# Feature tiles that pair heads of two units, in the linear-attention part of an attention and mixture-of-experts kernel

## The reference

```python
def taylor_feature_map(x):
    iu, ju = jnp.triu_indices(d)
    quad = x[..., iu] * x[..., ju] * scale
    return jnp.concatenate([ones, x, quad], axis=-1)
...
def step(carry, inp):
    kv, ksum = carry
    A = jnp.einsum('bchf,bshf->bhcs', qb, kb) * causal
    y = jnp.einsum('bhcs,bshd->bchd', A, vb) + jnp.einsum('bchf,bhfd->bchd', qb, kv)
    z = jnp.einsum('bhcs->bch', A) + jnp.einsum('bchf,bhf->bch', qb, ksum)
    kv = kv + jnp.einsum('bshf,bshd->bhfd', kb, vb)
    ksum = ksum + kb.sum(axis=1)
    return ((kv, ksum), y / (z[..., None] + EPS_LIN))
```

## Time and profile before

| what | us |
|---|---|
| median of three runs | 480.66 |
| profiled execution, whole | 480.37 |
| its span, first to last instruction | 478.6 |
| attention, first L640 to the last copy L839 | 49.0 to 282.1 |
| PE busy in the span | 406.1 |
| DVE busy | 290.9 |
| ACT busy | 206.2 |
| POOL busy | 179.2 |

### The profile page before, as it was taken

How to read it: one execution, slowest core, us unless ns; L and a number is a source line. 1 busy time by engine, 2 the same in 40 slices (tenths; PEclk the granted TensorE clock), 3 DMA queues, 4 the chain that set the end, 5 groups by cost and what they waited for, 6 DMA issues and landing times. The chain is left out here.

```text
span 478.6 us, 14438 instructions
## 1 busy us (share of the span) xinstructions
PE 406.1 (85%) x4869; PEld 272.9 (57%) x4869; DVE 290.9 (61%) x1178; ACT 206.2 (43%) x502; POOL 179.2 (37%) x305
## 2 busy tenths in 40 slices
PE   0787999999999999999999961599998999999830
PEld 0455777777776677777777640245555555555420
DVE  5575454667756667666675647256665666666614
ACT  0465455445554555554455530044444444444420
POOL 5444433454454554555544345003222222223220
PEclk9999999999999999999999995599999999999975
DMA  7556755444455444423223700211110111111008
GB/s 203 134 142 175 213 136 151 112 112 139 144 165 135 120 120 142 121 66 82 51 53 85 258 14 32 71 42 36 45 38 28 29 43 37 31 34 34 18 16 251
DMA packets 91624, 46.14 MB, mean 96 GB/s; under 512 B 56410, under 2 KB 89852, under 8 KB 91554
## 3 DMA queue, kind: packets, MB, share of 16 engines
q1 hardware_dynamic: 88562, 40.50, 31.8%
q0 software_dynamic: 2272, 4.46, 2.5%
q10 hardware_dynamic: 720, 0.26, 0.2%
HBM read 33.67 MB, written 11.98 MB: 95 GB/s over the span
## 5 line engine op out<-in xcount | busy, mean ns | idle before, releaser
L1097 DVE TENSOR_REDUCE mrow<-ps 128x4 f32<-128x512 f32 x64 | 44.2, 691 | 73.9 <-PE ps L604 73.9
L1303 POOL TENSOR_SCALAR_AFFINE_SELECT amat<-amat 128x512 f32<-128x512 f32 x64 | 42.1, 657 | 119.6 <-ACT amat L819 119.3
L1325 POOL DMA_INDIRECT results<-qas,mrowid x39 | 38.1, 978 | 126.2 <-ACT qas L879 123.1
L747 PE MATMUL ps<-wgl,rest 128*128 (+1 forms) x156 | 75.3, 605 | 4.7 <-DVE hT L1186 4.1
L830 ACT ACTIVATE pmat<-ps 128x512 f32<-128x512 f32 x64 | 38.2, 597 | 67.6 <-PE ps L661 67.6
L819 ACT ACTIVATE amat<-ps 128x512 f32<-128x512 f32 x64 | 38.2, 597 | 27.9 <-PE ps L616 27.9
L1186 DVE TENSOR_TENSOR hT<-ps,kv_tok 128x512 f32<-128x512 f32 x39 | 27.0, 691 | 26.5 <-issue 14.6
L747 PEld LDWEIGHTS ps<-wgl,rest 128*128 128x128 f32 x156 | 26.9, 192 | 27.9 <-issue 27.9
L732 PE MATMUL ps<-w,rest 128*128 (+1 forms) x78 | 42.1, 623 | 0.0
L661 PE MATMUL ps<-identb,mneg 128*128 128x128 bf16 x512 | 39.2, 219 | 0.0
L1264 POOL DMA_INDIRECT routed<-routed_row,slot x32 | 32.6, 1018 | 14.0 <-issue 5.8
(11 more groups left out here) (161 smaller groups left out, 834.7 us busy)
## 6 DMA issues: line engine op xcount, KB each, us to landing
qa_parts<-wgl SPq DMA_DIRECT2D x12, 256.0 KB, 3.1
ks<-k_parts SPq DMA_DIRECT2D x32, 96.0 KB
qas<-qa_parts SPq DMA_DIRECT2D x32, 96.0 KB
xin<-routed SPq DMA_DIRECT2D x39, 72.0 KB, 1.9
ks<-k_parts SPq DMA_DIRECT2D x32, 64.0 KB
qas<-qa_parts SPq DMA_DIRECT2D x32, 64.0 KB
w<-in_W SPq DMA_DIRECT2D x2, 1024.0 KB, 5.4
wgl<-in_Wg SPq DMA_DIRECT2D x2, 1024.0 KB, 6.3
```

The costliest lines, as they stand in the source:

```text
L747: t = mm(ps[:, GL, :], zxT[:, k % 2, s, :], rhs(wgl[:, bass.ds(e, 1), s, :]), start=(s == 0), stop=(s == 1))
L1097: v.tensor_reduce(mrow[:], ps[:, SQ, :].rearrange("p (a k) -> p a k", k=CH), AX.X, ALU.max).then_inc(max_done, 1)
L1303: q.affine_select(out=amat[:, u % 2], in_=amat[:, u % 2], compare_op=ALU.is_ge, fill=0.0, base=0, pattern=[[0, 4], [1, CH]], channel_multi ...
L1325: q.indirect_dma_start(results, bass.IndirectOffsetOnAxis(mrowid[:, m:m + 1], 0), yw[:, m, :], None, bounds_check=RESULTS - 1, oob_is_err= ...
```

## The change

Query features of a **pair** of units are now formed at once: tile g (0 to 3) holds head g of the even unit in its first 48 rows and head g of the odd unit in the other 48. L621 runs only before an even unit and writes 512 columns in each of its two products. ACT's square of it (L821) is 96 x 512, once for a pair. The product with `state` (L674 before) is done once for a pair, as four products with 32 weight columns, one for each g, whose outputs lie in the four groups of 32 output rows: the same groups that L679 uses. Keys follow: `u_tok` holds the heads in the new order, each product of L640 takes head g of both units of a pair (values with a stride), and DVE copies KV to `state` once for a pair, in the odd unit. The waits follow the new counts, and SP waits for the scores (`a_ready`) where it waited for the features (`phi_ready`).

```diff
@@ linear_scores
-                if not isinstance(n, int) or n:
-                    pe.wait_ge(phisq_done, n)
-                for par in range(2):
-                    t = mm(ps[0:PR, PHI, 0:2 * CH], sums[:, par, :], as_[:, p, 4 * u + par:4 * u + par + 3:2, :],
-                           start=par == 0, stop=par == 1)
-                t.then_inc(phi_ready, 1)
+                if u % 2 == 0:
+
+                    if n:
+                        pe.wait_ge(phisq_done, n // 2)
+                    for r in range(2):
+                        t = mm(ps[0:PR, PHI, :], sums[:, r, :], as_[:, p, 4 * (u + r):4 * (u + r) + 4, :], start=r == 0, stop=r == 1)
+                    t.then_inc(phi_ready, 1)
@@ chunk, TensorE
-                        if kf or u:
-                            pe.wait_ge(state_done, UNITS * kf + u)
-                        for k in range(2):
...
+                        if u % 2 == 0 and (kf or u):
+                            pe.wait_ge(state_done, 2 * kf + j)
+                        for g in range(2 * hf, 2 * hf + 2):
...
-                    pe.wait_ge(phisq_done, n + 1)
-                    if u % 2 == 0 and pair > 1:
-                        pe.wait_ge(evac_done, pair - 1)
...
-                    for k in range(2):
-                        t = mm(ps[64 * k:64 * k + 64, bank, 0:CH], slot32(state[:, c % 2], 4 * u + 2 * k, 2),
-                               phiq[:, u % 2, k, :], start=u % 2 == 0, stop=False, skip_group_check=True)
-                    t.then_inc(inter_done, 1)
+                    if u % 2 == 0:
+                        pe.wait_ge(phisq_done, pair + 1)
...
+                        for g in range(4):
+                            t = mm(ps[32 * g:32 * g + 32, bank, 0:CH], state[:, c % 2, j, 32 * g:32 * g + 32], phiq[:, pair % 2, g, :],
+                                   start=True, stop=False, skip_group_check=True)
+                        t.then_inc(inter_done, 1)
@@ squares, ScalarE
-                act.wait_ge(phi_ready, n + 1)
-                a_(phiq[:, u % 2].rearrange("p k t -> p (k t)"), ps[0:PR, PHI, 0:2 * CH], ACT.Square).then_inc(phisq_done, 1)
+                if u % 2 == 0:
+                    act.wait_ge(phi_ready, n // 2 + 1)
+                    a_(phiq[:, n // 2 % 2].rearrange("p g t -> p (g t)"), ps[0:PR, PHI, :], ACT.Square).then_inc(phisq_done, 1)
@@ next_state, VectorE
-                        if not later:
+                        if not later or u % 2 == 0:
                             return
@@ load_stack, SyncE
-                    sp.wait_ge(phi_ready, n + 4)
+                    sp.wait_ge(a_ready, n + 4)
```

More of the change, by code:

```diff
@@ L64, in constants @@
     c["blockdiag"] = (blk[:, None] == blk[None, :]).astype(np.float32)
-    sm = np.zeros((PR, 2, 2, UD), np.float32)
-    for par in range(2):
-        sm[par * FS:(par + 1) * FS, :, par] = 1.0
-    c["statemask"] = sm.reshape(PR, 4 * UD)
+    sm = np.zeros((PR, 4, 2, UD), np.float32)
+    for r in range(2):
+        sm[r * FS:(r + 1) * FS, :, r] = 1.0
+    c["statemask"] = sm.reshape(PR, 8 * UD)
     slots = np.zeros((128, 2 * H), np.float32)
@@ L129, in build @@
         blockdiag = sb("blockdiag", [D, D])
-        statemask = sb("statemask", [PR, 4 * UD])
+        statemask = sb("statemask", [PR, 8 * UD])
         epslin = sb("epslin", [128, 2 * H])
@@ L167, in build @@
         v1 = sb("v1", [CH, 2, 2, 2, SLOTW])
-        state = sb("state", [PR, 2, 2, SLOTW])
+        state = sb("state", [PR, 2, 2, CH])
         mrow = sb("mrow", [128, 4])
         mneg = sb("mneg", [128, 2, 2, 4], BF16)
-        phiq = sb("phiq", [PR, 2, 2, CH])
+        phiq = sb("phiq", [PR, 2, 4, CH])
         amat = sb("amat", [CH, 2, 4, CH])
@@ L286, in build, with slot32 @@
         TZX, X12, Y, TO, GL = SQ, ST, A, PHI, OUT0
-        def slot32(tile, h, heads=1):
+        def slot32(tile, h):
             lo = 128 * (h // 4 % 2) + 32 * (h % 4)
[L292 to L296, removed]
+            return tile[:, h // 8, lo:lo + 32]
         def values16(tile, lo, hi):
@@ L634, in chunk @@
                         pe.wait_ge(cross_ready, kf + 1)
-                        if kf or u:
-                            pe.wait_ge(state_done, UNITS * kf + u)
-                        for k in range(2):
[L638 to L642, removed]
+                        if u % 2 == 0 and (kf or u):
+                            pe.wait_ge(state_done, 2 * kf + j)
+                        for g in range(2 * hf, 2 * hf + 2):
+                            at = 4 * j + g
+                            t = mm(ps[0:PR, KV, 2 * at * UD:2 * (at + 1) * UD], phik[:, p, 2 * at:2 * at + 2, :].rearrange("p h f -> p (h f)"),
+                                   v1[:, p, 1, j, :].rearrange("p (r x) -> p r x", r=2)[:, :, 32 * g:32 * g + UD],
+                                   start=c % (T // CH) == 0 and at == 0, stop=True, skip_group_check=True)
                         t.then_inc(kv_ready, 1)
@@ L665, in chunk @@
                     bank = OUT0 + pair % 2
-                    pe.wait_ge(phisq_done, n + 1)
-                    if u % 2 == 0 and pair > 1:
-                        pe.wait_ge(evac_done, pair - 1)
[L669 to L672, removed]
-                    for k in range(2):
-                        t = mm(ps[64 * k:64 * k + 64, bank, 0:CH], slot32(state[:, c % 2], 4 * u + 2 * k, 2),
-                               phiq[:, u % 2, k, :], start=u % 2 == 0, stop=False, skip_group_check=True)
-                    t.then_inc(inter_done, 1)
+                    if u % 2 == 0:
+                        pe.wait_ge(phisq_done, pair + 1)
+                        if pair > 1:
+                            pe.wait_ge(evac_done, pair - 1)
+                        if c % (T // CH):
+                            pe.wait_ge(state_done, 2 * folded(c - 1)[1] + j + 1)
+                        elif c:
+                            pe.wait_ge(state_zeroed, 1)
+                        for g in range(4):
+                            t = mm(ps[32 * g:32 * g + 32, bank, 0:CH], state[:, c % 2, j, 32 * g:32 * g + 32], phiq[:, pair % 2, g, :],
+                                   start=True, stop=False, skip_group_check=True)
+                        t.then_inc(inter_done, 1)
                     pe.wait_ge(amask_ready, n + 1)
@@ L924, in key_features @@
                         dve.wait_ge(phik_ready, kf)
-                    v.tensor_copy(u_tok[:, :, 1:UD], kv_tok[:, c, 0, :].rearrange("p (h d) -> p h d", h=H)).then_inc(us, 1)
+                    v.tensor_copy(u_tok[:, :, 1:UD].rearrange("p (a g r) d -> p a r g d", a=2, g=4),
+                                  kv_tok[:, c, 0, :].rearrange("p (a r g d) -> p a r g d", a=2, r=2, g=4)).then_inc(us, 1)
                 for w in range(2):
@@ L1114, in next_state @@
                     def next_state():
-                        if not later:
+                        if not later or u % 2 == 0:
                             return
+                        a = u // 2
                         dve.wait_ge(kv_ready, UNITS * kf + u + 1)
                         if c:
[L1120 to L1123, removed]
+                            dve.wait_ge(inter_done, 2 * (c - 1) + a + 1)
+                        grf = lambda x: x.rearrange("p (g r f) -> p g r f", g=4, r=2)
+                        v.tensor_tensor(grf(state[:, (c + 1) % 2, a])[:, :, :, 0:UD], grf(ps[0:PR, KV, 8 * a * UD:8 * (a + 1) * UD]),
+                                        grf(statemask[:]), ALU.mult).then_inc(state_done, 1)
                     if n < UNITS * NC - 1:
@@ L1307, in chunk @@
                     if u == 0 and c == T // CH - 1:
-                        pool.wait_ge(inter_done, UNITS * c)
+                        pool.wait_ge(inter_done, 2 * c)
                         q.memset(state[:, (c + 1) % 2], 0.0).then_inc(state_zeroed, 1)
```

## The result

| | before | after |
|---|---|---|
| median of the runs, us | 480.25 (478.96 to 481.72, 4 runs) | 468.45 (467.94 to 469.27, 4 runs) |
| profiled execution, us | 480.37 | 469.27 |
| span, us | 478.6 | 467.1 |

The ratio is 0.9734, 95% interval 0.9704 to 0.9764: 11.8 us faster, against 469.0 forecast, inside the range of 457 to 472. The two profiled executions differ by 11.1 us.

A forecast was written before the change was run, and what follows sets the result against it. PE's own sequence was taken to bound the attention (98% busy). Its 16.7 us saving, cut by holds at chunk borders to 11.3 (5.2 + 5.4 + 0.7), took 480.37 to 469.0 us, range 457 to 472.

The forecast's parts named there:

- L674 in the odd unit: State product on PE in odd units: it goes and nothing replaces it, saving 0.37 us a pair.
- L674 in the even unit: State product joined to L679: one handover (0.37) goes, two sets at 0.11 come, saving 0.15 us a pair.
- L621, nothing: Feature sums, halved in number, doubled in width: even units save 0.22 us, odd ones add 0.22; removed weight loads were hidden.
- The rule of the Trainium skill: Weight loads overlap matmuls only when row groups differ; 64 exposed loads would add 5.8 us saved: 463, chance 0.04.
- The hold, anchored to POOL's chain: Chunk start: L557's wait ends with POOL's indirect DMA, 5.44 us after L616 of u = 2; held chunks give 0.54, not 1.04.
- the time of that exponential: In u = 0 ACT's exponential ends at 212.15, so L691 saves only 0.24 us where it would be 0.37 earlier.
- the tenth border: Chunk 7 to 8: PE 0.44 us earlier against the DMA, hold 0.69 longer (1.24), so the hold ends with the DMA.
- the first rival: Chunk borders: the hold vanishes because L691 ends before the DMA blocks anything; 22.9 us less, 457.5, chance 0.3.
- PE waits for no load: In the attention, SP's later wait costs nothing: the loads queued behind it are for a chunk 15 us away.
- wrong in kind: Sign in the changed kernel's profile that the forecast fails: PE waits for `phiq`, `state` or a load.
- The forecast of 11.3: Total saving in us: five chunks without hold 5.2, ten held 5.4, chunk 15 0.7.
- 16.7 us from PE: Saving on PE if nothing else holds it: 0.52 us a pair, 1.04 a chunk, 32 pairs.

The follow-up runs named there:

- the run with the wide sums alone: Kernel before with feature sums and their square made once per pair of units, state product still one per unit: 473.43 us against 473.67, ratio 0.9975.

## Why the forecast came out right

**L674 in the odd unit, 0.37 a pair: right.** L678 follows L659 directly.

**L674 in the even unit, 0.15 a pair: right.** 0.58 measured for the 0.57 worked out, and the middle set that the trace before did not show costs 0.11, as taken from L621 and L691. The rows left it anywhere between 0.06 and 0.16; the value between was a choice, and it held.

**L621, nothing: right.** L614 to L690 takes 0.33 and 0.76 where 0.33 and 0.77 were worked out, and the run with the wide sums alone is level with the kernel before. The rule of the Trainium skill that spoke against it ("TensorE: Matmul & The Clock Gate", part 3, "The mechanism") has no support here: four loads and two take the same time to 0.01 us.

**The hold, anchored to POOL's chain: right where it stood, and nine times, not ten.** L614 of u = 2 stands at 197.44 and L555 at 202.87:

```profile
197.44 0.40 PE L614 MATMUL ps<-qas,ks 114*128 114x128 bf16 x4
```

That is 5.43, and the forecast had it stay at 5.44. Of the 1.04 us of a chunk, 0.6 was left in six of these nine chunks and 0.35 to 0.50 in three, 0.56 on the mean; 0.54 was forecast. The 0.08 that L614 to L690 takes too long in u = 0 (0.41, the exponential) is part of it, smaller than the 0.13 forecast. The forecast took the time of that exponential as given; it was late because the DMA of u = 0 held the signal that starts it.

**The forecast's reading of the tenth border was wrong.** At chunk 7 to 8 I took the late DMA for a proof that an earlier PE waits longer. There the hold went altogether:

```profile
158.62 0.43 PE L690 MATMUL ps<-pmat,v 128*32 128x64 f32 x16
...
159.37 1.07 POOL L1266 DMA_INDIRECT routed<-routed_row,slot  x1 [0.20 <-issue]
...
159.26 0.26 ACT L838 COPY linT<-ps 128x128 f32<-128x128 f32 x1
```

L690 ended at 159.05, before the DMA began at 159.37, and ACT had copied by then. So the first rival happened once, and gave 2.3 us in that chunk instead of 0.54. The forecast's argument for that rival, that L621's signal passed while the DMA ran, was sound as a reading and did not decide it. Elsewhere L690 ended inside the DMA (201.25 against 201.13) and was held.

**Two smaller misses took that gain back.** First, I said that PE waits for no load. In chunk 1 it did:

```profile
73.20 0.42 PE L602 MATMUL ps<-ks,qas 114*64 114x128 bf16 x8 [0.73 <-issue]
...
75.21 0.38 PE L614 MATMUL ps<-qas,ks 114*128 114x128 bf16 x4 [0.44 <-issue]
```

In u = 3 these are the first steps that read the next chunk's loads; from L614 to L614 that unit took 3.94 us instead of 2.62. By the forecast's own words this is wrong in kind, though for one chunk and 1.3 us. That it is the load the trace shows: the last packet of the queries that L602 reads landed at 73.11, that of the keys that L614 reads at 75.12, each 0.09 before the step. SP had issued them at 66.66 and 69.03, so they took 6.5 and 6.1 us to land. The change brings PE there 0.8 us earlier (it would start at 72.40, where the kernel before started at 73.20), but that is not enough by itself: in the same kernel without the hold SP issued the same two at 67.22 and 70.16, later, they landed at 71.98 and 72.92, and PE did not wait. Nor does the wait need the hold, for the trace of the kernel with one DMA moved, in a group without it, has it too, and longer; there the queries were issued at 70.27 and landed at 74.10:

```profile
74.19 0.41 PE L602 MATMUL ps<-ks,qas 114*64 114x128 bf16 x8 [1.72 <-issue]
```

Second, the border from chunk 6 to 7, where I had counted no hold, got one: 4.44 us from L614 to L614 there, where 3.74 was free of it at the same border in a group without the hold. The indirect DMA comes earlier in those chunks (no key products ahead of it), and it now falls on L614 of u = 3.

**The sum.** By chunks, in the profiled execution: 1.3 in chunk 0, -0.3 in chunk 1, 1.05 each in 2 and 3, 5.1 in the nine held ones, 0.5 in chunk 7 (border 6 to 7), 2.3 in chunk 8 (border 7 to 8): 11.0. With the last chunk the attention saved 11.4 from its first linear scores to its last copy (282.10 - 47.75 before, 271.86 - 48.90 after). The prologue was 1.1 longer, the way from the last copy to the first expert tile 0.7 longer, and the experts' part 1.9 shorter, none of it touched by the change. The forecast of 11.3 was close partly because these errors have both signs: the terms on PE were right to 0.02 us each, the count and size of the holds was not. And it was luck that the change was first timed in a group with the hold, like the trace that the forecast was read from: in a group without, the same two kernels are 17.0 us apart. What would have been a safer statement is the one the later groups gave: 16.7 us from PE if nothing is held, less 0.4 to 0.7 for every border that an indirect DMA holds.

What stays open is what turns the hold on. By their times all runs of a group agree on it; the groups do not, even on one chip. Nor do the traces say why some of TensorE's signals pass during the DMA and others do not.

## What to carry to other kernels

Work on TensorE from start to start: a group costs a handover plus its columns, so merging two groups of one shape, or dropping a group whose outputs can go into a neighbour's, pays a whole handover, while halving a count at the same number of columns pays nothing. Before adding up what a faster engine saves, look for the waits in the same loop that do not run on that engine; here a chain on GpSimd ended in an indirect DMA, and where that DMA held, 0.4 to 0.7 us of the 1.04 us saved in a chunk was lost. And moving such a DMA to where no signal is waited for is worth trying by itself: it gave 1.2% on the kernel before where the hold stood, 4.9% together with this change and one chunk's earlier loads, and nothing where the hold did not stand. Time the kernel before again beside each change: here its own level moved by 1.8%.

## What the runs showed of the hardware that was not expected

- In some groups signals from TensorE that fell to an indirect DMA issue on GpSimd were raised only after it: 0.75 us late at a border (L691's end at 208.64, raised at 209.39, copy at 209.41), up to 1.45 us in one case (L691's end at 163.06), while TensorE itself went on with its next groups. In other groups the same program started the copy 0.21 us after L691's end, in the middle of the DMA. The other engines' signals were not late but for two, in one of the four traces with the hold.
- The same kernel took 473.4 us in one group of runs and 481.8 in a later one on the same chip. Of such a difference 6.6 us lie between the first linear scores and the last (230.2 us in the first trace, 223.6 in one without the hold), and the ten holds of 0.55 to 1.24 at the borders, 6.2 us in all, are most of them.
- A set of four 32-column f32 products with 128 columns to stream costs 0.11 us between other sets of its shape, with 96 rows in use (L673).
- Loads of the same size took 6.1 to 6.5 us from issue to landing in one trace and 2.8 to 4.8 in another, and PE waited in the first.
